# Row normalisation moved from VectorE to GpSimd in a fused FFN, recurrence and FFN kernel, with new group sizes and pacing

## What is computed

```python
x = L0_attn_x                                                     # 16 x 512 x 128, float32
x = x + 0.5 * ffn(layernorm(x), router_w, expert_fc, expert_proj)
x = x + rnn(layernorm(x), Wi, bi, Wh, bh)
x = x + 0.5 * ffn(layernorm(x), router_w, expert_fc, expert_proj)

def ffn(x, ...):   # 8 experts, the one with the largest logit x @ router_w.T is used
    h = square(relu(x @ expert_fc[e]))                            # 128 -> 512
    return h @ expert_proj[e].T                                   # 512 -> 128
def rnn(x, ...):   # 512 dependent steps, batch 16
    h = tanh(x[:, t] @ Wi.T + bi + h @ Wh.T + bh)
```

## Time and profile before

| | us |
|---|---|
| median of 3 executions | 612.68 |
| lowest, highest | 606.79, 624.44 |
| the profiled execution, its own time | 603.88 |
| its span, first to last instruction | 602.0 |

### The profile page before, as it was taken

The page is one execution under the profiler, slowest core; times in us unless marked ns, Lnnn a source line. Parts: engine busy times, 40 slices in busy tenths (PEclk is TensorE's granted clock), DMA queues, the critical chain, the costliest instruction groups (busy, mean ns, idle before and its releaser), DMA issues.

```text
span 602.0 us, 16237 instructions
## 1 busy us (share of the span) xinstructions
PE 551.4 (92%) x4714; PEld 533.7 (89%) x4714; DVE 412.8 (69%) x1507; ACT 315.4 (52%) x1089; POOL 423.5 (70%) x520
## 2 busy tenths in 40 slices
PE   7799798997999989999999999998999999869991
PEld 6798698897999989999999999997889999658991
DVE  5789867886667878657876774577546466665661
ACT  2133165464666546666666666654346666425660
POOL 2699497789995778978874987838849638664552
PEclk9889999998999999999999999999999999998997
DMA  5977432221222223322321532101152301435310
GB/s 184 296 273 289 109 105 81 79 78 59 78 80 69 66 82 97 93 68 63 98 81 49 132 111 77 39 27 68 45 144 76 84 20 69 139 115 151 101 37 1
DMA packets 54163, 58.89 MB, mean 98 GB/s; under 512 B 8999, under 2 KB 42034, under 8 KB 54080
## 3 DMA queue, kind: packets, MB, share of 16 engines
q1 hardware_dynamic: 44064, 36.68, 21.0%
q0 software_dynamic: 9440, 21.06, 10.8%
q10 hardware_dynamic: 576, 0.13, 0.1%
HBM read 27.67 MB, written 30.62 MB: 97 GB/s over the span
## 4 chain that ended last, share of the span: by engine, by line
PE 74%; DVE 11%; issue 7%; DMA 2%; SPq 1%; ACT 1%; another core or an unknown queue 1%; ACTq 0%; POOLq 0%; DVEq 0%
PE yp L1687 23%; PE hp L1677 20%; PE z L1697 11%; PE mT L1583 4%; PE lg L1627 3%; PE xTp L1666 3%; PE hp L1702 3%; DMA hsT<-in_L_attn_x_dram 2%; PE z L1647 2%; PE yp L1707 2%; DVE pay L1238 2%; DVE r_sb L1361 2%; PE hp L1616 1%; SPq L1012 1%
## 5 line engine op out<-in xcount | busy, mean ns | idle before, releaser
L1687 PE MATMUL yp<-projT,s_sb 128*128 x1248 | 198.3, 291 | 11.6 <-ACT s_sb L1495 5.9
L1677 PE MATMUL hp<-xT_sb,w_sb 128*128 128x128 f32 x1248 | 193.2, 286 | 2.0 <-DVE xT_sb L1355 1.3
L1687 PEld LDWEIGHTS yp<-projT,s_sb 128*128 128x128 f32 x1248 | 161.3, 194 | 14.6 <-issue 14.2
L1466 ACT ACTIVATE hsT<-z 128x16 f32<-128x16 f32 x512 | 93.5, 183 | 147.5 <-PE z L1697 102.7
L1677 PEld LDWEIGHTS hp<-xT_sb,w_sb 128*128 128x128 f32 x1248 | 161.7, 193 | 3.1 <-DVE xT_sb L1355 1.4
L1697 PEld LDWEIGHTS z<-hsT,wT 128*128 128x128 f32 x1024 | 154.0, 190 | 8.9 <-ACT hsT L1466 3.0
L1697 PE MATMUL z<-hsT,wT 128*128 128x16 f32 x1024 | 158.0, 230 | 1.4 <-ACT hsT L1466 1.2
L1495 ACT ACTIVATE s_sb<-r_sb 128x256 f32<-128x256 f32 (+1 forms) x252 | 115.7, 461 | 74.5 <-issue 51.8
L1361 DVE TENSOR_SCALAR r_sb<-hp 128x512 f32<-128x512 f32 x156 | 106.9, 686 | 66.6 <-PE hp L1677 55.9
L1152 POOL MEMSET idle<- 128x600 f32 x187 | 116.0, 620 | 0.2
L1189 POOL DMA_INDIRECT out_dram<-y_sb,xs_sb x71 | 70.1, 988 | 61.7 <-DVE y_sb L1368 34.9
(11 more groups left out here) (132 smaller groups left out, 564.3 us busy)
## 6 DMA issues: line engine op xcount, KB each, us to landing
xs_sb<-xs_dram SPq DMA_DIRECT2D x71, 129.0 KB
xs_sb<-xy_dram SPq DMA_DIRECT2D x85, 64.0 KB
xy_dram<-y_sb SPq DMA_DIRECT2D x85, 64.0 KB
xy_dram<-zeros SPq DMA_DIRECT2D x10, 512.0 KB, 6.0
hsT<-in_L_attn_x_dram SPq DMA_DIRECT2D x16, 256.0 KB
hsT<-n_L_ffn_expert_proj_dram SPq DMA_DIRECT2D x2, 1024.0 KB
fc_sb<-in_L_ffn_expert_fc_dram SPq DMA_DIRECT2D x1, 2048.0 KB
out_dram<-y_sb,xs_sb POOLq DMA_INDIRECT x71
```

The costliest lines, as they stand in the source:

```text
L1466: act.activation(state(t), z_step(t), ACT.Tanh).then_inc(s_h, 1)
L1677: mm = pe.matmul(hp[:, g % 2, h * P:(h + 1) * P], w_sb[:, g % 2, h * P:(h + 1) * P], xT_sb[:, g % 2, :], start=True, stop=True)
L1687: mm = pe.matmul(yp[:, 0:D], s_sb[:, g % 2, h, :], projT[:, bass.ds(offsets[g] + h * D, D)], start=(h == 0), stop=(h == HC - 1))
```

## The change

VectorE's `normalise` is gone. GpSimd has `normalise_row`, one instruction per row, and `pool_order` holds a `norm` entry for every row: the rows of a scattered group are normalised one ahead of the scatter, between two scatters; the rows between first FFN and recurrence all after their `root`. A scatter no longer waits for VectorE's normalised rows to be queued, but must come behind its group's `root`. Pauses stand wherever the planner's pace of 1.75 us per indirect DMA asks for one, also after the last recurrence step. The first group is 4 units instead of 5, the second 4 instead of 3; the lists of all three groups are staged by single units; the middle and second groups are other ones (nine instead of eight second groups); all 25 weights of the planner are other numbers. Two of the first four input loads are issued by ScalarE instead of SP.

```diff
-FIRST = [5, 3, 8]
-STEP = [1, 3, 1]
-MIDDLE = [1, 1, 1, 1, 1, 1, 1, 1, 1, 1, 3, 3]
-SECOND = [3, 2, 2, 3, 2, 2, 1, 1]
+FIRST = [4, 4, 8]
+STEP = [1, 1, 1]
+MIDDLE = [1, 1, 1, 1, 1, 1, 1, 1, 1, 2, 3, 1, 1]
+SECOND = [4, 3, 1, 2, 1, 2, 1, 1, 1]
+PACE = 1.75
-PR = {'proj': -38.387, 'lat1': 30.338, 'lat2': 69.811, 'lat3': -18.484, 'last': 24.985,
+PR = {'proj': 76.794, 'lat1': 229.681, 'lat2': 50.506, 'lat3': -53.201, 'last': -341.658,
...
-AHEAD = [4, 5, 7]
+AHEAD = [4, 5, 5]
...
             if what in ("root", "mroot"):
+                pool_order.append(p[1])
                 pool_free = start + 0.7 + 0.16 * key.J
                 ev[p[1]] = pool_free + 0.05
+                for j in range(key.J if what == "mroot" else 1):
+                    pool_order.append(("norm", key, j))
+                    pool_free += NORM
...
+            if what == "scatter" and p[1][2] + 1 < key.J:
+                pool_order.append(("norm", key, p[1][2] + 1))
+                start += NORM
+            while REST and drained > start + PR["burst"]:
+                pool_order.append(("rest",))
+                start += REST / 1250
+            pool_order.append(p[1])
...
+            def normalise_row(r, j):
+                n, w = r.n0 + j, 2 if isinstance(r, Middle) else int(r.second)
+                if j == 0:
+                    pool.wait_ge(s_root, root_no["mroot" if w == 2 else "root", r.index])
+                pool.tensor_scalar(pay[:, n, XN:XN + D], row_in(w, n), mv[:, w, n, 0:1], rstd[:, w, n:n + 1],
+                                   ALU.subtract, ALU.mult).then_inc(s_row, 1)
...
-                if j % 4 == 0:
-                    pool.wait_ge(s_norm, 4 * norm_no["norm", r.index, j // 4])
+                pool.wait_ge(s_row, row_no[r, j])
...
-            def normalise(what, c, i):
-                w = 2 if what == "mnorm" else int(c.second)
-                dve.wait_ge(s_root, root_no["mroot" if what == "mnorm" else "root", c.index])
-                for n in range(c.n0 + 4 * i, c.n0 + 4 * i + 4):
-                    dve.tensor_scalar(pay[:, n, XN:XN + D], row_in(w, n), mv[:, w, n, 0:1], rstd[:, w, n:n + 1],
-                                      ALU.subtract, ALU.mult).then_inc(s_norm, 1)
...
+            for u in range(min(FIRST[0], NU // 2)):
+                if by_act(u):
+                    act.dma_start(raw(u), x[:, u * UNIT:(u + 1) * UNIT, :].rearrange("b (th j) d -> th b (j d)", j=UR)
+                                  ).then_inc(s_in[u], 16)
...
-                    pe.wait_ge(s_norm, 4 * norm_no["mnorm", m.index, key - m.u0])
+                    pe.wait_ge(s_row, row_no[m, UR * (key - m.u0) + UR - 1])
```

83 lines of the change are left out of this document (41 added, 42 removed).

## The result

The changed kernel takes 670.25 us (median of 4 runs, 660.02 to 672.57), the kernel before 609.85 us on the same chip. The ratio is 1.097, 95% interval 1.086 to 1.109: slower by almost 10%. The forecast was 591 us, with a range of 577 to 607. The profiled run took 672.57 us, its span is 670.8 us. Executions of one kernel differ by up to a few per cent with the clock that TensorE was granted, so the ratios in this document compare the faster executions of each kernel, and the profile shown here is of an execution 12 us above the fastest.

What follows compares the result with a forecast made beforehand. The recurrence stage was taken as TensorE-bound, the start as set by VectorE. Start 58.5, to first step 55.4, steps 380.0, after 77.3, closing 9.6 gave 580.8 us span, scaled by ratio 0.965 to 591 us; range 577 to 607.

Steps and rivals of the forecast that it cites:

- N is one normalisation ... I take 0.43: Price of one 128-column normalisation on GpSimd: 0.43 us, the middle between a select's 0.29 and an extrapolated 0.56.
- the cycle: GpSimd's time from scatter to scatter in the start: DMA 0.97, gap 0.17 and one normalisation, 1.57 us together.
- The rest of the sum: Stage times: start 58.5, to first step 55.4, steps 380.0, after them 77.3, closing 9.6; span 580.8 us.
- The same 12.8 us of waits: Between first and last recurrence step, TensorE's waits were taken as unchanged at 12.8 us.
- 69 us of room hide it: GpSimd's work of 513 of some 582 us leaves 69 us spare, said to hide the moved normalisations.
- signs of being wrong: GpSimd DMAs ending TensorE's waits, normalisation above 0.8 us, first step still at 119, or closing stage over 12 us.
- Groups and weights at no cost of their own: New groups, order and planner weights: the forecast sum carried no separate loss for them.
- The start: Time to the first expert product, set by VectorE: 58.5 instead of 69.5 us, a gain of 11.0.
- The second limit: GpSimd's first gather at about 89 us would allow the first step at 112.5, just inside 113.9 us.
- Pauses behind the last step, 0: The added GpSimd pauses after the last recurrence step cost nothing: 0, ends -2 and +6 us.
- GpSimd late in places: Rival: late scatters or puts make TensorE wait, +14 us, median 605; chance 0.21.
- GpSimd sets the end: Rival: GpSimd's sum, 430 + 192 N, passes the forecast's 582 us at N = 0.79; chance 0.10.

Runs made afterwards that it cites:

- e12b: Repeat, on another chip, of the changed kernel with each GpSimd normalisation replaced by a select and a one-column memset (0.41 us a row): 599.15 us, ratio 0.983.
- e12: The changed kernel, same order, each GpSimd normalisation replaced by a select and a one-column memset (0.41 us a row): 596.61 us, ratio 0.979.
- e19: The changed kernel, same order, each GpSimd normalisation replaced by a select and two one-column memsets: 600.60 us, ratio 0.984.
- e7: The changed kernel without the pauses behind the last recurrence step, all else as it is: 663.99 us, ratio 1.115.
- e8: The changed kernel with 128 added TensorE products that fill its waits for middle units' rows: 654.98 us, ratio 1.076.
- e13: The kernel before with pauses until the end, also behind the last recurrence step: 609.02 us, ratio 1.018.
- e11: The changed kernel with real normalisations and each GpSimd pause cut from 600 to 60 columns: 714.79 us, ratio 1.160.
- e4: Apparently the kernel before with the changed one's groups and weights, normalisations on VectorE, planned anew (label not spelled out): 640.16 us, ratio 1.055.

## Why the prediction was wrong, by its own steps

- **"N is one normalisation ... I take 0.43", bounds 0.29 and 0.56: the step that failed.** It measured 0.81, outside both bounds. The upper bound was a line drawn through scalar operations of 4 and 32 columns and stretched to 128; from 32 to 128 columns the measured slope is 3.2 ns a column even with one operand (0.312 to 0.62 us), not 2.6, and two per-partition operands add 0.15 us more (0.66 to 0.81). The lower bound, the select, is another operation: 0.30 here, less than half. With the DMA at 1.07 behind a row, the cycle is 2.1 us, not 1.57. The Trainium skill's page GPSIMD Engine Reference, section 3.1 Elementwise, has GpSimd 1.96 times slower than VectorE in an addition of two inputs, and gave an estimate of 0.66 us in the prediction; the run with constants agrees (0.66), the real operands exceed it, and both lie outside the bounds that the sum went by. The page's figure was nearer than the rows that the sum chose, though it is of another operation too (two inputs, 2048 columns), so that it came so near is partly luck.
- **The rest of the sum held, where the clock was high.** With a row at 0.41 us the profile (e12b) has: first product at 63.5, at 56.8 in the same kernel's other profile (forecast 58.5), then 57.7 us to the first step (55.4), 383.2 us of steps (380.0), and a span of 584.3 against the forecast 580.8. Only the part behind the last step was 7 us too long in the forecast (79.9 against 77.3 + 9.6). But e12b's profile had a clock of 0.98 in the steps; e12's and e19's, with 0.94 and 0.91, have 397 and 410 us of steps. The medians are 597 to 601 us, the ratios 0.979, 0.983 and 0.984 (0.99 to 1.00 between the medians): at the forecast's own price the gain would have been 0 to 2%, not 3.5%.
- **"The same 12.8 us of waits": failed as a consequence.** Idle time between the steps is 40.7 us, and 23.5 us of it are waits for GpSimd's rows. "69 us of room hide it" is the reasoning behind it: room in a total is not room in a place. A middle unit's way goes through GpSimd (gathers 1.73 us apart, root, four rows of 0.81), and a share of 83% over the whole span says nothing of it. Two of the prediction's signs of being wrong came true here: a normalisation above 0.8 us, and a first step later than 119 (128.3); a third came in another form, as GpSimd's rows, not its gathers or scatters, ended TensorE's waits.
- **The clock was in no step.** It is the largest part, 54 of 79 us in the profiles shown and 40 of 64 with e7's in place of the changed kernel's. The waits that the earlier trace rows showed had a clock of 1.00 around them, and I carried the price of waiting as the waiting alone. Here 24 to 25 us of added waits came with 40 to 54 us of slower work, and not all of that is their doing (e19 above).
- **Groups and weights at no cost of their own**: right in this order, as e12 and e19 show. **The start**, 11.0 us from VectorE's path: 59.5 against 58.5 in the profile; but the fourteen profiles with this order of TensorE (the added products of e8 aside) start between 57 and 71 us, by how long TensorE ran at half clock. The match to 1 us is luck: kind against kind, the gain is 5 to 13 us (69.3 against 57 to 64) or 4 to 12 (75 against 63 to 71). The second limit did pass it: the first gather at 106 us instead of 89 set the first step at 128.3. **Pauses behind the last step, 0**: right (e7, e13).
- **The rivals.** "GpSimd late in places", +14 us, had the mechanism and a fifth or sixth of the size (its waits are 25 us, the clock is missing). "GpSimd sets the end" named the point from which things turn, N = 0.79, and N passed it, but its price, the engine's plain sum, would be 430 + 192 x 0.81 = 586 us; the time is far above, because GpSimd too waits for what it delays (POOL veps for VectorE's statistics, 19.7 us, puts for y_sb, 12.1).

## What to carry to other kernels

Before arithmetic moves to another engine, its price there needs a row of the same operation, the same operands and the same width; a line through smaller sizes and a row of another operation are no bounds. An engine's spare time counts only where its work stands directly in front of the engine that sets the time, and a wait of TensorE is to be priced with the clock that can be lost behind it: 3.0 us of waiting for a row was followed by 34 us at half clock here, two waits of 1.4 us by none. Before two profiles are compared, see what clock each had: products of one form, timed in both, show it even where the clock column does not. Where GpSimd sends many indirect DMAs, the spacing between them is part of the design: making GpSimd faster can make everything slower.

## What the runs showed of the hardware

- TensorE's half clock outlasts the wait in front of it: after 3.0 us of idle time at 318 to 321 us the granted clock was 0.53 and 0.62 over the next 40 us while TensorE was busy 97% of them, and 1.00 again later. It is not in proportion to the wait: none behind two waits of 1.4 us, 34 us behind one of 3.0. Work put into such waits lifted the mean clock from 0.87 to 0.94 (e8). It also comes without added waits: e19, with 15.4 us of idle time between the steps, had 0.91 there, e12b with 15.3 us 0.98.
- At its start TensorE runs at half clock, in some executions up to about 11 us, in others up to 25 us or more, with all the work it can take (e7: eight products 1.72 us, later 0.96). The profile's clock column shows 1.00 there.
- Twelve indirect DMAs of GpSimd 1.28 us apart stalled hand-offs between the other engines by up to 7 us (e11), and bursts of four to six at the end of the kernel before by up to 3.6 us; bursts of seven at the end of e4 and e7 did not. At 1.73 us none was seen; at 1.50 us it was seen in two kernels on one chip, and not in a third kernel on two other chips.
- GpSimd at 128 columns of float32: 0.81 us with two per-partition operands, 0.66 with two constants, 0.62 with one operand and one operation, 0.30 for a select, 0.10 for a memset of one column. An indirect DMA behind such a scalar operation takes 1.05 to 1.07 us, behind a select or a memset 0.99.
